# Self-attention on one Trainium2 core: TensorE's list of a tile goes from scores, transposes, values product, transposes, projection to scores, transposes, projection, transposes, values product

## The reference

```python
q = (x @ Wq).reshape(b, n, h, d).transpose(0, 2, 1, 3)   # h = 16 heads, d = 64
...
dots = jnp.einsum('bhid,bhjd->bhij', q, k) * scale
dots = dots + _rel_bias(rel_emb, n)[None]
attn = jax.nn.softmax(dots, axis=-1)
out = jnp.einsum('bhij,bhjd->bhid', attn, v)
```

## Time and profile before

| | |
|---|---|
| time of the kernel, median of 3 runs | 2169.19 us (2168.51 to 2175.8) |
| the profiled execution | 2169.09 us, with a span of 2167.3 us in the trace |
| tiles of self-attention, start of the first scores to start of the last | 49.91 to 887.20 us |
| TensorE busy over the span | 94%, granted clock 0.97 |
| VectorE, ScalarE, GpSimd busy over the span | 64%, 48%, 45% |

### The profile page before, as it was taken

How to read it: one execution, slowest core, us unless ns; L and a number is a source line. 1 busy time by engine, 2 the same in 40 slices (tenths; PEclk the granted TensorE clock), 3 DMA queues, 4 the chain that set the end, 5 groups by cost and what they waited for, 6 DMA issues and landing times.

```text
span 2167.3 us, 54537 instructions
## 1 busy us (share of the span) xinstructions
PE 2030.5 (94%) x22465; PEld 1686.3 (78%) x22465; DVE 1392.1 (64%) x3108; ACT 1047.6 (48%) x2108; POOL 978.8 (45%) x762
## 2 busy tenths in 40 slices
PE   6999999999999999869999779999999999998994
PEld 4677777777777777558888669999989999988883
DVE  6666666666666666447887776555466455456983
ACT  3666666666666666414544444234245334324551
POOL 1555555555555555414545343433334334344441
PEclk9999999999999999969999899999999999999996
DMA  7001020101010101202131111000121010030000
GB/s 270 6 18 47 21 96 15 55 11 54 11 55 11 47 11 41 102 31 71 41 107 44 49 34 53 22 12 13 29 91 51 17 32 17 17 123 25 11 16 15
DMA packets 59990, 97.16 MB, mean 45 GB/s; under 512 B 7720, under 2 KB 50480, under 8 KB 57392
## 3 DMA queue, kind: packets, MB, share of 16 engines
q1 hardware_dynamic: 57184, 86.69, 12.0%
q10 hardware_dynamic: 2560, 6.99, 0.8%
HBM read 70.45 MB, written 23.20 MB: 43 GB/s over the span
## 4 chain that ended last, share of the span: by engine, by line
PE 42%; DVE 7%; issue 4%; ACT 2%; POOL 2%; DVEq 0%; POOLq 0%; ACTq 0%
PE psum L262 12%; PE psum L273 10%; PE psum L1814 4%; PE psum L243 2%; PE psum L1802 2%; PE psum L2306 2%; PE psum L1788 2%; PE psum L1143 1%; DVE b_act L1375 1%; PE psum L222 1%; PE psum L1130 1%; PE psum L2340 1%; DVE b_acc L1383 1%; ACT e_pr L2445 1%; POOL b_act_lo L1287 1%
## 5 line engine op out<-in xcount | busy, mean ns | idle before, releaser
L761 POOL TENSOR_TENSOR a_sm<-a_sm,a_rsum 128x1024 f32<-128x1024 f32 x256 | 485.2, 1895 | 391.2 <-DVE a_rsum L793 389.2
L781 DVE CUSTOM_DVE_ANT_0 a_sm<-psum,a_strip 128x1024 f32<-128x1024 f32 x256 | 312.0, 1219 | 57.9 <-PE psum L621 57.9
L700 ACT ACTIVATE a_sm<-a_sm,a_mn 128x1024 f32<-128x1024 f32 x256 | 293.6, 1147 | 24.2 <-DVE a_mn L781 24.1
L634 PEld LDWEIGHTS psum<-ident,a_sm 128*128 128x128 f32 x2048 | 218.9, 141 | 101.0 <-issue 92.9
L705 ACT ACTIVATE a_pT<-psum 128x512 f32<-128x512 f32 x256 | 153.0, 598 | 283.5 <-PE psum L634 283.4
L634 PE MATMUL psum<-ident,a_sm 128*128 128x128 f32 x2048 | 279.6, 280 | 4.7 <-POOL a_sm L761 4.6
L649 PE MATMUL psum<-a_pT,a_V 128*64 128x256 f32 x2048 | 249.0, 385 | 0.8 <-DVE a_pT L788 0.8
L788 DVE COPY a_pT<-psum 128x512 f32<-128x512 f32 x256 | 176.3, 689 | 101.5 <-PE psum L634 101.5
L649 PEld LDWEIGHTS psum<-a_pT,a_V 128*64 128x64 f32 x2048 | 136.2, 136 | 77.3 <-issue 21.1
L1898 ACT ACTIVATE g_val<-psum 128x512 f32<-128x512 f32 x64 | 38.1, 597 | 219.4 <-PE psum L1814 219.4
L1287 POOL TENSOR_TENSOR b_act_lo<-b_act,b_act_hi 128x512 fp32r<-128x512 f32 x64 | 91.2, 1430 | 102.2 <-ACT b_act_hi L1185 102.2
(11 more groups left out here) (329 smaller groups left out, 4234.4 us busy)
## 6 DMA issues: line engine op xcount, KB each, us to landing
a_strip<-table SPq DMA_DIRECT2D x16, 960.0 KB, 6.5
oT<-a_o SPq DMA_DIRECT2D x64, 128.0 KB, 1.9
b_oT_in<-oT SPq DMA_DIRECT2D x8, 1024.0 KB, 5.5
a_raw<-in_a_wqkv SPq DMA_DIRECT2D x7, 384.0 KB, 3.3
s_x<-in_x_rev SPq DMA_DIRECT2D x4, 512.0 KB, 7.4
vb<-s_zero SPq DMA_DIRECT2D x8, 256.0 KB, 2.7
b_x_in<-in_x SPq DMA_DIRECT2D x8, 256.0 KB, 5.6
b_vb_in<-vb SPq DMA_DIRECT2D x8, 256.0 KB, 5.4
```

The lines of the kernel that those rows point to most:

```text
L634: last = pe.transpose(psum[:, 4 + j, k * P:(k + 1) * P], sm[:, st % RING, kt * P:(kt + 1) * P], ident[:, :])
L700: a.activation(sm[:, st % RING, :], sm[:, st % RING, :], ACT.Exp, scale=-1.0, bias=mn[:, at:at + 1], accum_out=rsum[:, at:at + 1]).then_in ...
L761: g.tensor_tensor(sm[:, st % RING, :], sm[:, st % RING, :], rsum[:, at:at + 1].broadcast_to([P, T]), ALU.mult).then_inc(sig("scaled"), 1)
L781: v.tensor_tensor_reduce(out=sm[:, st % RING, :], in0=scores_banks(hl).rearrange("p c n -> p (c n)"), in1=strip[:, pair % 2, hl, qt * P:qt ...
```

## The change

The order of four calls in TensorE's list of a tile is changed. No instruction is added or removed, and the lists of the other engines and of the DMA queue stay as they are.

```diff
                     if n + 1 < NI:
                         scores(n + 1)
                     transposed(n, 0)
+                    if NU + n < len(units):
+                        project(NU + n)
+                    transposed(n, 1)
                     if n > 1:
                         values(n // 2 - 1, n % 2)
-                    transposed(n, 1)
-                    if NU + n < len(units):
-                        project(NU + n)
                 values(NG - 1, 0)
                 values(NG - 1, 1)
```

## The result

The changed kernel took 2159.08 us (median of 7 runs, 2152.56 to 2164.39) against 2174.18 us for the kernel before (7 runs, 2168.51 to 2183.25). The ratio is 0.9928, with a 95% interval of 0.9911 to 0.9946: 15.6 us less, 11.7 to 19.4 (the plain difference of the two medians is 15.1). The forecast was 15.7 us less. In absolute time it was 2153.5 us, counted down from the 2169.19 us of the first three runs of the kernel before; with seven runs that kernel's median is 5 us higher, and the changed kernel's is 5.6 us above the forecast, inside its range of 2148 to 2163. The profiled execution took 2152.56 us with a span of 2150.7 us, 16.6 us less than the one before. From the first scores to the last values matmul the stage took 852.7 us before (49.91 to 902.58) and takes 837.9 us now (50.06 to 887.99).

A forecast was written before the change was run, and what follows sets the result against it. TensorE's own list was taken to bound self-attention. Full tiles -17.0, first tiles -2.7 and last tiles +4.0 sum to -15.7 us, from 2169.1 us profiled to 2153.4, as a median 2153.5 us; range 2148 to 2163.

The forecast's parts named there:

- Steps 1 to 3: Full tiles: projection to transposes 0.09 us less, second transposes 0.055 less, values to scores 1.88; over 117 tiles 17.0 us less.
- Step 4: Waits met by the earlier second transposes: slack before the fifth 0.15 us (v), 0.67 (q, k); put at no cost.
- the rival of the late copy: VectorE's copy of bank 5 delays the fifth transpose in tiles with v, taking back 6 to 12 us; chance 0.13.
- Step 5: First tiles: the projection fills the wait for GpSimd's late product, so the fourth tile's scores start 2.7 us earlier.
- Step 6: Last tiles, without projection: second transposes wait for the banks, tiles take 6.10 us instead of 5.53; 4.0 us lost in all.
- Values to scores: Rival: scores behind the values product take 2.14 us instead of 1.88, 32 us more over 123 tiles; chance 0.04.
- the seams: Rival: savings at changes of shape are lost at a new place, full tiles keep 6.92 and 6.39 us; chance 0.06.
- that rival: Clock falls in the last eight tiles after transposes, a wait and transposes, costing 13 to 27 us; chance 0.04.

The follow-up runs named there:

- e5: Changed kernel with the values product moved ahead of both heads' transposes, still three changes of shape in a tile; ratio 1.0156 to the kernel before.
- e3: Kernel before with each values product cut in two around the second head's transposes, six changes of shape instead of four; ratio 1.0184 to the kernel before.
- e1: Changed kernel with the values product moved ahead of the second head's transposes, four changes of shape in a tile; ratio 1.0048 to the kernel before.
- e7: Changed kernel with VectorE's copy of bank 5 moved behind both bias operations; ratio 1.0394 to the kernel before.
- e8: Kernel before with VectorE's copy of bank 5 moved behind both bias operations; ratio 0.9978 to the kernel before.
- e4: Kernel before with the new order in tiles 0 and 1 only; 2170.33 us in a single run, against a median of 2172.99 us for the kernel before.
- e10: Changed kernel with the old order in the last eight tiles; 2152.27 us, ratio 0.9889 to the kernel before.

## Why the prediction was right

**What bounds the stage.** TensorE's own list did, and still does. The full tiles had no wait in the list before and have none after.

**Steps 1 to 3, the changes of shape.** These held. For tiles with q or k 0.145 us had been worked out and 0.15 measured (6.92 to 6.77), with each of the new seams as forecast: 1.48 us for projection to transposes, 1.88 for values to scores. The last was the one without a row; it costs what the other changes of shape cost. That the number of changes is the cause was shown from three sides: one fewer between other neighbours gives the same tile (e5), two more add 0.34 us and one more 0.13 (e3), and as many as before give the time of before (the tiles with v in e1).

**Step 4, the waits.** The slack at the fifth transpose was put at 0.15 us for tiles with v, and at no cost. That held: the transposes around it stand at their usual pace (the third to the sixth in the last row here). What was mis-sized is "a piece of v I take to save the same". Behind a piece of v the second transpose comes 0.14 us after the first (0.41 less 0.27), behind a piece of q or k 0.11:

```profile
396.21 0.41 PE L634 MATMUL psum<-ident,a_sm 128*128 128x128 f32 x2
115.89 0.38 PE L634 MATMUL psum<-ident,a_sm 128*128 128x128 f32 x2
396.46 0.60 PE L634 MATMUL psum<-ident,a_sm 128*128 128x128 f32 x4
```

So tiles with v gained 0.13 us and not 0.145. In e5, with other waits in the tile, the second transpose behind a piece of v comes just as late; why is open. The 117 full tiles together took 777.8 us before (76.12 to 853.93) and 761.3 after (73.43 to 834.76): 16.5 us less, for 17.0 forecast. How near the rival of the late copy was, e7 and e8 show: one bias operation (1.2 us) more ahead of the copy costs some 100 us under the new order.

**Step 5, the first tiles.** 2.7 us forecast; 2.8 measured from the first to the fifth scores (26.2 and 23.4 us), and 2.9 in e4, where nothing else was changed. But about half of it is not the order's. The prediction read the granted clock as full throughout the stage, since a slice of the earlier trace rows is 54 us long; in the kernel before it was 0.57 from 66 to 70 us (the last figure but two of the first row here; the later rows are e3's). The kernel of e3 has the list of before in tiles 0 and 1, the same wait for GpSimd in front of the second head's transposes of tile 1, and a clock of 1.00 in that stretch:

```profile
66.00:70.00 4.00, 4.00 (x16) 2.81 (x16) 1.14 (x3) 2.27 (x4) 3.34 (x2) 0.57 0.00 0
```

```profile
66.77 1.09 PE L634 MATMUL psum<-ident,a_sm 128*128 128x128 f32 x8 [1.95 <-POOL a_sm L766]
67.61 1.18 PE L669 MATMUL psum<-a_hT_hi,a_W 128*128 128x512 f32 x4
...
69.19 0.49 PE L621 MATMUL psum<-a_KH,a_QH 64*128 64x512 f32 x2
```

From these transposes to the next scores 2.4 us pass (66.77 to 69.19), against 3.7 in the kernel before (65.25 to 68.97). With the slow first scores of the next tile the clock cost 1.5 us in that one execution, and the order is worth about 1.3 us. The forecast was read from the same execution that it is compared with here, so that 2.7 came out is in part luck. Nor does the new order keep the clock up: e10 starts with the same list as the changed kernel, its granted clock was 0.51 from 56.0 to 59.4 us, and from its first scores to the fifth 24.0 us pass instead of 23.4. How often either kernel meets this is not known, with a profile or two of each.

**Step 6, the last tiles.** 4.0 us forecast, 4.6 measured: the six intervals from 853.93 to 887.20 us (33.3) became 37.3 (834.76 to 872.04), 4.0 where 3.4 had been put, and the end 0.57. One of the six is 6.50 us long, with a wait of 0.4 us for VectorE's copy. The mechanism is the one named: VectorE's copy lets the fifth transpose go 3.69 us after the tile's scores (840.91 to 844.60), where 3.68 had been worked out. TensorE's list names ScalarE's copy in these tiles, for the first four transposes, but that wait is over sooner and doesn't set the tile. The 0.06 us between 6.10 and 6.16 lie behind it: the first two transposes after the wait take 0.44 us (844.60), so the second comes 0.17 us after the first and not 0.11, though the shape of the array stays. So the part of the price that was read at the first start of a new shape is paid after such a wait as well.

**The sum.** In the stage -2.8 - 16.5 + 4.6 = -14.7 us, against -15.7. Without the 1.5 us of the clock it would be 13.2 us. The measured ratio gives -15.6 +- 4, so the runs can't tell the two apart; the traces can.

**The rivals.** Values to scores was not dear, and the seams did give their gain. The granted clock of the changed kernel was 1.00 from 50 to 888 us, the last tiles included. The row on which that rival rested, half pace after transposes, a wait of 1.9 us and transposes, doesn't repeat in e3.

## What to carry to other kernels

When TensorE never waits and its list still takes longer than its matmuls' pace, read the starts around every place where the array's shape changes (whole, split by rows, split by columns), and order the list so that groups of one shape stand together: here that was worth 0.13 to 0.15 us for each change saved. Then check each wait that the moved groups meet, bank by bank, against the time at which they now arrive; a group that comes 0.6 to 1.1 us earlier spends slack that other orders of VectorE's list rely on. And where the loop's last or first turns lack one of the groups, look at them apart: the old order was better in eight of 128 tiles, and keeping it there gave another 4 us. Before a gain at one place is credited to an order, read the granted clock of just that stretch in both traces.

## What was not expected

- An early projection with late second transposes (e1) is worse than either order: the bank that all projections share is emptied by a chain that runs from the second transposes over ScalarE's copy, the exponentials and two copies of the bank. It cost 0.24 us in each tile behind one with q or k.
- The values product ahead of the transposes (e5) waits up to 0.7 us for its own bank in every second tile, 26.2 us in all; the copy of that bank stands on ScalarE behind a tile's exponentials.
- The runs of one kernel lie up to 15 us apart on one chip (2167.15 to 2182.10 us for the kernel before beside e5 to e8), while the full tiles' times agree within 0.02 us from trace to trace; parts of the sum as small as those of the first and last tiles can only be read in the timeline.
